# Indirect transfers without padding rows in the last tiles of a graph kernel

## The chip, the cores and the metric

The kernel runs on 1 core of one Trainium2 chip. The metric is the device time in microseconds (us), median of the runs shown. A core has a matrix engine (PE), a vector engine (DVE), a scalar engine (ACT), a general engine (POOL, GpSimd) and a queue engine (SP). Direct DMAs are issued from SP here, indirect ones (gather or scatter by a list of row numbers) from POOL; both run on the core's 16 DMA engines.

## The reference

One layer of attention over the edges of a graph, with a residual and a normalization: 100,000 nodes of 128 float32, 25,000 edges.

```python
dst, src = (edge_index[0], edge_index[1])      # receiver and sender of each edge
edge_feat = concatenate([h[dst], h[src], rel_pos, distance], axis=-1)
x = silu(edge_feat @ W1 + b1)
x = silu(x @ W2 + b2)
scores = (x @ W3 + b3)[:, 0]
mx = segment_max(scores, dst, num_segments=num_nodes)
exp_scores = exp(scores - mx[dst])
den = segment_sum(exp_scores, dst, num_segments=num_nodes)
alpha = exp_scores / (den[dst] + EPS)
msg = h[src] @ Wv * (alpha * node_weight[src])[:, None]
out = segment_sum(msg, dst, num_segments=num_nodes)
return layernorm(x0 + h + out)                 # h is x0, the input
```

## The kernel before

The 25,000 edges are cut into T = 196 tiles of P = 128 edges, four tiles to a group, G = 49 groups. 196 tiles hold EP = 25,088 edges, so 88 places are padding. The padding's sender is node 0, and its receiver is N, past the last node; all 88 come at the end of the edge list, in the last tile, which holds 40 real edges.

The work has three stages, all laid out by hand as a list of steps for each engine:

- Stage 1 (to about 270 us). For each group POOL gathers the senders' rows (`xw`: 128 values and the node's weight, 516 bytes) by `snd_t` into `rec` (kind "hs"); PE transposes them (line 584) and multiplies by the sender half of W1 and by the edge features (lines 577, 578); ACT copies the product beside the gathered row (line 493); SP writes the record of 257 values to `rec_d` in DRAM (`write_rec`, line 343). Beside it DVE sorts the edges by receiver (a sorting network over 98 rows of 256), which gives the tables `id_t`, `kg_t`, `sidx_t` of edge number, receiver and output row. In sorted order the padding again comes last.
- Stage 2 (to about 790 us). In sorted order POOL gathers the receivers' rows of `x` by `kg_t` into `hk` (kind "hk", 512 bytes) and the records by `id_t` into `rr` (kind "r", 1,028 bytes; the profile calls its memory `region`). PE, ACT and DVE compute scores, a softmax over each receiver's run of edges, and the weighted sums, 12 to 13 steps behind; ACT normalizes the finished rows in `hk` (line 530).
- Stage 3. POOL scatters the rows of `hk` by `sidx_t` into `out_rows` (kind "sc", line 426). Only the last edge of a run carries an output row; the other rows go to spare rows of `out_rows` past row N, one for each edge. Runs that cross tiles are combined for all tiles at once and scattered by two closing transfers (line 430): 196 rows, one for each tile, as 128 and 68; both transfers handle 128 rows, and a row whose index is past the bound (`SKIP`) is not written.

Beside stages 1 and 2 the nodes without edges are normalized: SP loads and stores 49 blocks of 1 MB, ACT and DVE normalize them.

POOL's order is fixed by `pool_plan`: all 49 groups "hs"; ten groups "hk"; then "r" and "hk" in turn, and when "hk" is out, the last ten groups of "r" in a row; then 49 groups "sc"; then the closing two. A group is always four transfers of one tile each. POOL waits before a group: "hs" for its place in a ring of 12 (`rec_out`); the first "hk" for the sorted tables; the first "r" for all records written; "r" of group g for the product of line 645 of group g - 12 (`z_ready`); "sc" for the dense rows written, then for its group's result (`res_ready`).

Of the kernel before, what the change touches and what calls it, by code (L numbers as in the profile page):

```python
# [11 lines left out]
P = 128  # L12
N = 100000
E = 25000
H = 128
# [4 lines left out]
T = G * TPG  # L20
XW = H + 1
RW = 2 * H + 1
# [2 lines left out]
NB = -(-N // BN)  # L25
LASTROW = N - BN
NOUT = N + 1 + EP

HS_RING, EF_RING, R_RING, X_RING = 12, 4, 12, 4
HK_SEMS, SC_SEMS, Y_SEMS, FAR_RING = 16, 8, 4, 4  # L30
# [22 lines left out]
SKIP = float(1 << 20)  # L53
MAGIC = float(0x5F3759DF)
FLAT = (T + BT) * P
assert SROWS * SORTW == EP and T <= SORTW and EP < 1 << IDBITS and SROWS < P
assert (HALFN - POSB) >> 8 > 0 and NEGB < 255 << 8 and N - POSB < 255 << 8 and (NEGB - HALFN + 1) >> 8 > 0

# [60 lines left out]
def gnn_kernel(nc, x, xw, snd_nat, rcv_nat, id_nat, signs, iota, ef_flat, w1, b1, w2, b2, w3, b3, wv, eye, out):  # L119
    rec_d = nc.dram_tensor("rec_d", (EP, RW), F32).ap()  # L120
    ef_d = nc.dram_tensor("ef_d", (36, EP), BF16).ap()
    far_d = nc.dram_tensor("far_d", (1, FLAT + P), BF16).ap()
    cont_d = nc.dram_tensor("cont_d", (1, FLAT + P), BF16).ap()
# [6 lines left out]
    with ExitStack() as ctx:  # L130
# [6 lines left out]
        ident = sb("ident", [P, P])  # L137
# [8 lines left out]
        snd_t = sb("snd_t", [P, T], I32)  # L146
        id_t = sb("id_t", [P, T], I32)
        kg_t = sb("kg_t", [P, T], I32)
        sidx_t = sb("sidx_t", [P, T], I32)
        kcol = sb("kcol", [P, T])  # L150
        krow = sb("krow", [P, KROW_RING, GE], BF16)
        fixi = sb("fixi", [P, 2], I32)

        hk = sb("hk", [P, G, TPG, H])
# [12 lines left out]
        dst = sb("dst", [P, BR, 3])  # L167
# [6 lines left out]
        rr = region[:].rearrange("p (r q w) -> p r q w", r=R_RING, q=TPG)  # L174
        at = [0]
# [6 lines left out]
        ef = part(EF_RING * GE // 2).bitcast(BF16).rearrange("p (r e) -> p r e", r=EF_RING)  # L182
# [11 lines left out]
        rec = hflat[:, G * GE - HS_RING * TPG * RW:].rearrange("p (r q w) -> p r q w", r=HS_RING, q=TPG)  # L194
# [35 lines left out]
        fv = late(T)  # L230
        fw = late(T)
        yfix = late(2 * H).rearrange("p (k h) -> p k h", k=2)
        yrow = late(4 * H).rearrange("p (k h) -> p k h", k=4)
        fixf = late(2)

        bank = [ctx.enter_context(nc.psum_tensor(f"bank{n}", [P, GE], F32)) for n in range(8)]
# [10 lines left out]
        hs_in = [sem(f"hs_in{r}") for r in range(HS_RING)]  # L247
        ef_in = [sem(f"ef_in{r}") for r in range(EF_RING)]
        rec_out = [sem(f"rec_out{r}") for r in range(HS_RING)]
        r_in = [sem(f"r_in{r}") for r in range(R_RING)]  # L250
        hk_in = [sem(f"hk_in{r}") for r in range(HK_SEMS)]
# [5 lines left out]
        scattered = [sem(f"scattered{r}") for r in range(SC_SEMS)]  # L257
# [33 lines left out]
        def _(sp):  # L291
# [105 lines left out]
                        sp.wait_ge(stored[r], 16 * len(range(r, NB, X_RING)))  # L397
                    sp.sem_inc(S["dense_written"], 1)
            sp.dma_start(fara, fara_d.to_broadcast((P, T))).then_inc(S["fix_in"], 16)
            for k, (first, n) in enumerate(((0, P), (P, T - P))):  # L400
                sp.dma_start(fixf[0:n, k:k + 1], fixi_d[0:1, first:first + n].rearrange("o t -> t o")).then_inc(S["fix_in"], 16)
            sp.wait_ge(S["parts_ready"], 1)
            for k in range(4):
# [14 lines left out]

        @block.gpsimd
        def _(pool):  # L420
            def gather(to, frm, index, done):
                pool.indirect_dma_start(out=to, out_offset=None, in_=frm,  # L422
                                        in_offset=bass.IndirectOffsetOnAxis(ap=index, axis=0)).then_inc(done, 16)

            def scatter(frm, index, done):
                pool.indirect_dma_start(out=out, out_offset=bass.IndirectOffsetOnAxis(ap=index, axis=0),  # L426
                                        in_=frm, in_offset=None).then_inc(done, 16)

            def scatter_some(frm, index, done):
                pool.indirect_dma_start(out=out, out_offset=bass.IndirectOffsetOnAxis(ap=index, axis=0),  # L430
                                        in_=frm, in_offset=None, bounds_check=N - 1, oob_is_err=False).then_inc(done, 16)

            pool.wait_ge(S["snd_in"], 16)
            for kind, g in pool_plan():
                if kind == "hs":
                    wait_ring(pool, rec_out, g - HS_RING, 16)
                    for q in range(TPG):
                        t = g * TPG + q
                        gather(rec[:, g % HS_RING, q, H:RW], xw, snd_t[:, t:t + 1], hs_in[g % HS_RING])
                elif kind == "hk":  # L440
                    if g == 0:
                        pool.wait_ge(S["tab_ready"], 1)
                        pool.wait_ge(S["efp_out"], 144)
                        pool.wait_ge(S["w36_in"], 144)
                    wait_ring(pool, hk_in, g - HK_SEMS, 16 * TPG)
                    for q in range(TPG):
                        t = g * TPG + q
                        gather(hk[:, g, q, :], x, kg_t[:, t:t + 1], hk_in[g % HK_SEMS])
                elif kind == "r":
                    if g == 0:  # L450
                        for r in range(HS_RING):
                            pool.wait_ge(rec_out[r], 16 * len(range(r, G, HS_RING)))
                        pool.wait_ge(S["rows_out"], 80)
                    wait(pool, "z_ready", g - R_RING + 1)
                    for q in range(TPG):
                        t = g * TPG + q
                        gather(rr[:, g % R_RING, q, :], rec_d, id_t[:, t:t + 1], r_in[g % R_RING])
                else:
                    if g == 0:
                        pool.wait_ge(S["dense_written"], 1)  # L460
                    wait(pool, "res_ready", g + 1)
                    wait_ring(pool, scattered, g - SC_SEMS, 16 * TPG)
                    for q in range(TPG):
                        t = g * TPG + q
                        scatter(hk[:, g, q, :], sidx_t[:, t:t + 1], scattered[g % SC_SEMS])
            pool.wait_ge(S["fix_res"], 1)
            for k in range(2):
                scatter_some(yfix[:, k, :], fixi[:, k:k + 1], S["fix_out"])


        @block.scalar
# [72 lines left out]
        def _(pe):  # L544
# [24 lines left out]
            for i in range(B0):  # L569
                j = i - 2  # L570
                if 0 <= j < G:
# [3 lines left out]
                    for q in range(TPG):  # L575
                        to = bank[2 + j % 4][:, q * P:(q + 1) * P]
                        pe.matmul(to, hsT[:, j % 2, q * P:(q + 1) * P], w1b[:], start=True, stop=False)  # L577
                        ins = pe.matmul(to, ef[0:36, j % EF_RING, q * P:(q + 1) * P], w36[:], start=False, stop=True)  # L578
                    ins.then_inc(S["A_ready"], 1)
                if i < G:  # L580
                    wait_ring(pe, hs_in, i, 16 * TPG)
                    wait(pe, "hsT_ready", i - 1)
                    for q in range(TPG):
                        ins = pe.transpose(bank[i % 2][:, q * P:(q + 1) * P], rec[:, i % HS_RING, q, H:2 * H], ident[:])  # L584
# [16 lines left out]
            for s in range(LAST_STEP):  # L601
                g = s - 3
                if 0 <= g < G:
# [3 lines left out]
                    for q in range(TPG):  # L607
                        n = (g % BATCH) * TPG + q
                        ins = pe.matmul(bank[3][0:BT, 0:P], wz[:, BT - 1 - n:2 * BT - 1 - n], x2[:, q * P:(q + 1) * P],  # L609
                                        start=(n == 0), stop=(last and q == TPG - 1), skip_group_check=True)  # L610
                    ins.then_inc(S["score_done"], 1)
                g = s - 2
# [4 lines left out]
                g = s - 1  # L617
                if 0 <= g < G:
# [4 lines left out]
                    for q in range(TPG):  # L623
                        ins = pe.matmul(bank[1][:, q * P:(q + 1) * P], rr[:, g % R_RING, q, 0:H], ident[:], is_transpose=True,  # L624
                                        start=False, stop=(q == TPG - 1), skip_group_check=True)
                    ins.then_inc(S["mm1_done"], 1)
                for b in range(NBATCH):
                    if batch_end(b) + 5 == s:
                        n = group_tiles(b)
# [3 lines left out]
                g = s - Z_LAG - 1  # L633
                if 0 <= g < G:
                    wait(pe, "zs_ready", g + 1)
                    wait(pe, "y_done", g - 1)
                    for q in range(TPG):
                        ins = pe.matmul(bank[Y_BANKS[g % 2]][:, q * P:(q + 1) * P], zs[:, q * P:(q + 1) * P], wvh[:], start=True, stop=True)  # L638
                    ins.then_inc(S["y_ready"], 1)
                g = s - Z_LAG  # L640
                if 0 <= g < G:
                    wait(pe, "m_ready", g + 1)
                    wait(pe, "zs_ready", g)
                    for q in range(TPG):
                        ins = pe.matmul(bank[5][:, q * P:(q + 1) * P], rr[:, g % R_RING, q, H:2 * H], m_q[:, g % 2, q, :],  # L645
                                        start=True, stop=True)
# [5 lines left out]
            for k in range(2):  # L652
                pe.transpose(bank[k][:, 0:P], yrow[:, 2 * k, :], ident[:])
                ins = pe.transpose(bank[k][:, P:T], yrow[0:T - P, 2 * k + 1, :], ident[0:T - P, 0:T - P])
            ins.then_inc(S["fixT_done"], 1)
            pe.wait_ge(S["fixY_ready"], 1)
            pe.transpose(bank[2][:, 0:P], fv[:, 0:P], ident[:])
            pe.transpose(bank[2][0:T - P, P:2 * P], fv[:, P:T], ident[:]).then_inc(S["fixY_done"], 1)


        @block.vector
        def _(dve):
            vec = nc.vector
            count = [0]

            def link(ins):
                count[0] += 1
                ins.then_inc(S["setup"], 1)
                dve.wait_ge(S["setup"], count[0])
# [316 lines left out]
            for s in range(LAST_STEP):  # L986
# [14 lines left out]
                for b in range(NBATCH):  # L1001
                    if batch_end(b) + 4 == s:
                        softmax_first(b)
                    if batch_end(b) + 6 == s:
                        wait(dve, "alphaT_done", b + 1)
                        n, first = group_tiles(b), b * BATCH % R_RING
# [42 lines left out]
            link(vec.reciprocal(h_, h_))  # L1049
            vec.tensor_tensor(fv, fv, h_, ALU.mult).then_inc(S["fixY_ready"], 1)  # L1050
            link(vec.memset(fixi[:], int(SKIP)))
            vec.tensor_copy(fixi[:, 0:1], fixf[:, 0:1])
            link(vec.tensor_copy(fixi[0:T - P, 1:2], fixf[0:T - P, 1:2]))
            dve.wait_ge(S["fixY_done"], 1)
            vec.tensor_copy(yfix[:, 0, :], bank[2][:, 0:P])
            link(vec.tensor_copy(yfix[0:T - P, 1, :], bank[2][0:T - P, P:2 * P]))
            vec.bn_stats(est[:, 1, 0:2, :].rearrange("p j w -> p (j w)"), yfix.rearrange("p j h -> p h j")).then_inc(S["fix_stats"], 1)
            dve.wait_ge(S["res_ready"], G)
            for _ in chain(("fix_stats", 1), 2, est[:, 1], ers[:, 1], cwe, "chain_f", 0, lambda: None):
# [55 lines left out]
```

## Time and profile before

| | us |
|---|---|
| three runs | 998.05, 998.94, 999.92 |
| median | 998.94 |
| profiled execution, span from first to last instruction | 996.1 |
| POOL busy in it | 752.3 (76%) |
| PE busy | 575.9 (58%) |
| DVE busy | 573.2 (58%) |
| ACT busy | 522.6 (52%) |

The profiled execution is known by its span alone; what lies around the span is in the time of a run and not in the span. Busy time leaves out an engine's gaps between two instructions, so an engine that is never asked to wait can stand well below 100%. The DMA engines are nearly full to about 280 us and almost empty from 743 us on.

### The profile page before, as it was taken

The page shows a single profiled execution, that of the slowest core. Times are in us where ns is not written, and L with a number is a line of the kernel's source. Part 1 is how long each engine was busy: PE and PEld are TensorE (multiplying, and loading weights), DVE is VectorE, ACT ScalarE, POOL GpSimd, SP SyncE. Part 2 cuts the span into 40 slices and gives each one's busy share as a digit, 9 for nine tenths or more (in the row PEclk, how much of TensorE's full clock was granted, in tenths as well). Part 3 has the DMA queues.
Part 4 walks back from the last instruction along what each step waited for, and adds up shares of the span by engine and source line. Part 5 has one row for each costly group of instructions (what it writes and reads, how often), then busy time and mean ns, then how long its engine had stood idle before and what let it go on. Part 6 is the DMA issues. An engine that isn't in the chain of part 4 may idle for free.

```text
span 996.1 us, 10941 instructions
## 1 busy us (share of the span) xinstructions
PE 575.9 (58%) x2587; PEld 394.8 (40%) x2587; DVE 573.2 (58%) x2275; ACT 522.6 (52%) x1168; POOL 752.3 (76%) x790
## 2 busy tenths in 40 slices
PE   0989999988704457677667666777996600000000
PEld 0656766665502223455445444545675500000000
DVE  6987887773452737597698987953678841000000
ACT  0356655554523756777698979974786630000000
POOL 6777777777777777777777777777777777777777
PEclk9999999999998776788788988878999855555555
DMA  7799999989965877788778878763452231111111
GB/s 208 227 302 315 321 320 333 336 233 311 330 226 161 288 256 245 273 292 268 273 272 283 292 234 317 246 185 91 129 124 79 71 78 53 53 51 52 53 53 45
DMA packets 85079, 206.12 MB, mean 207 GB/s; under 512 B 19797, under 2 KB 56566, under 8 KB 72472
## 3 DMA queue, kind: packets, MB, share of 16 engines
q1 hardware_dynamic: 56728, 140.95, 41.7%
q0 software_dynamic: 28288, 64.48, 22.8%
q8 instruction: 21, 0.34, 0.1%
q14 instruction: 42, 0.34, 0.1%
HBM read 113.16 MB, written 92.31 MB: 206 GB/s over the span
## 4 chain that ended last, share of the span: by engine, by line
POOL 38%; issue 23%; PE 20%; ACT 13%; DVE 5%; DMA 0%; POOLq 0%; ACTq 0%; DVEq 0%
POOL hk L422 23%; POOL out_rows L426 15%; ACT xin L478 6%; PE bank L622 5%; PE bank L638 4%; PE bank L645 3%; PE bank L624 2%; ACT hk L530 2%; PE bank L616 2%; PE bank L609 2%; ACT hkT L501 1%; ACT x L511 1%; ACT zs L521 1%; PE bank L597 1%; DVE dst L899 1%
## 5 line engine op out<-in xcount | busy, mean ns | idle before, releaser
L478 ACT ACTIVATE xin<-xin,drs 128x128 f32<-128x128 f32 x637 | 258.1, 484 | 51.6 <-DVE drs L884 51.5
L422 POOL DMA_INDIRECT hk<-in_xw,snd_t x196 | 188.0, 959 | 62.0 <-issue 59.4
L426 POOL DMA_INDIRECT out_rows<-hk,sidx_t x196 | 188.8, 963 | 59.7 <-issue 59.4
L422 POOL DMA_INDIRECT region<-rec_d,id_t x196 | 186.8, 953 | 59.7 <-issue 59.1
L422 POOL DMA_INDIRECT hk<-in_x,kg_t x196 | 186.6, 952 | 59.7 <-issue 59.7
L899 DVE BATCH_NORM_STATS2 dst<-xin 128x6 f32<-128x256 f32 x392 | 137.0, 414 | 61.6 <-DMA xin<-in_x 61.0
L577 PE MATMUL bank<-w1b,region 128*128 128x128 f32 x392 | 149.1, 484 | 13.8 <-ACT region L488 7.8
L622 PE MATMUL bank<-hkT,w1a 128*128 128x512 f32 x98 | 73.2, 839 | 138.8 <-issue 98.3
L577 PEld LDWEIGHTS bank<-w1b,region 128*128 128x128 f32 x392 | 99.8, 315 | 33.9 <-ACT region L488 10.1
L622 PEld LDWEIGHTS bank<-hkT,w1a 128*128 128x128 f32 x98 | 20.1, 240 | 175.5 <-issue 163.2
L511 ACT ACTIVATE x<-bank,bcol 128x512 f32<-128x512 f32 x49 | 33.5, 683 | 95.0 <-PE bank L624 95.0
L530 ACT ACTIVATE hk<-hk,ers 128x128 f32<-128x128 f32 x196 | 79.6, 483 | 0.8 <-DVE ers L884 0.8
L488 ACT ACTIVATE region<-bank 128x512 f32<-128x512 f32 x49 | 28.9, 589 | 91.4 <-PE bank L584 91.4
L584 PE MATMUL bank<-ident,hk 128*128 128x128 f32 x196 | 54.3, 433 | 21.6 <-DMA w<-hk 16.8
L638 PE MATMUL bank<-wvh,zs 128*128 128x128 f32 x392 | 63.7, 314 | 4.1 <-ACT zs L521 4.1
L967 DVE TENSOR_SCALAR m_q<-krow,kcol,acol 128x128 f32<-128x128 bf16 x196 | 62.4, 354 | 4.6 <-PE bank L645 4.4
L609 PE MATMUL bank<-x,wz 128*16 128x128 f32 x392 | 55.5, 289 | 15.4 <-ACT x L506 9.6
L616 PE MATMUL bank<-x,w2s 128*128 128x512 f32 x98 | 59.0, 686 | 6.8 <-ACT x L511 4.7
L638 PEld LDWEIGHTS bank<-wvh,zs 128*128 128x128 f32 x392 | 57.8, 226 | 6.3 <-ACT zs L521 5.5
L645 PE MATMUL bank<-m_q,region 128*128 128x128 f32 x392 | 57.6, 296 | 0.0
L578 PE MATMUL bank<-w,region 36*128 36x128 bf16 x196 | 55.6, 284 | 0.0
L645 PEld LDWEIGHTS bank<-m_q,region 128*128 128x128 f32 x392 | 54.5, 215 | 0.0
(176 smaller groups left out, 853.0 us busy)
## 6 DMA issues: line engine op xcount, KB each, us to landing
xin<-in_x SPq DMA_DIRECT2D x49, 1024.0 KB, 8.2
out_rows<-xin SPq DMA_DIRECT2D x49, 1024.0 KB, 5.2
rec_d<-hk SPq DMA_DIRECT2D x49, 514.0 KB, 7.7
krow<-seg_d SPq DMA_DIRECT2D x49, 128.0 KB, 3.5
hk<-in_xw,snd_t POOLq DMA_INDIRECT x196, 5.8
hk<-in_x,kg_t POOLq DMA_INDIRECT x196, 3.9
region<-rec_d,id_t POOLq DMA_INDIRECT x196, 3.6
out_rows<-hk,sidx_t POOLq DMA_INDIRECT x196, 2.2
```

What stands on the lines that cost most here:

```text
L422: pool.indirect_dma_start(out=to, out_offset=None, in_=frm, in_offset=bass.IndirectOffsetOnAxis(ap=index, axis=0)).then_inc(done, 16)
L426: pool.indirect_dma_start(out=out, out_offset=bass.IndirectOffsetOnAxis(ap=index, axis=0), in_=frm, in_offset=None).then_inc(done, 16)
L478: ins = nc.scalar.activation(xin[:, j % X_RING, n, :], xin[:, j % X_RING, n, :], ACT.Identity, bias=drs[:, j % 2, 1, n:n + 1], scale=drs[: ...
L530: ins = nc.scalar.activation(hk[:, g, q, :], hk[:, g, q, :], ACT.Identity, scale=ers[:, b % 2, 0, n:n + 1], bias=ers[:, b % 2, 1, n:n + 1])
L577: pe.matmul(to, hsT[:, j % 2, q * P:(q + 1) * P], w1b[:], start=True, stop=False)
L609: ins = pe.matmul(bank[3][0:BT, 0:P], wz[:, BT - 1 - n:2 * BT - 1 - n], x2[:, q * P:(q + 1) * P], start=(n == 0), stop=(last and q == TPG ...
L616: pe.matmul(bank[2][:], w2s[:], x1[:], start=True, stop=True).then_inc(S["mm2_done"], 1)
L622: pe.matmul(bank[1][:], w1a[:], hkT[:, g % 2, :], start=True, stop=False, skip_group_check=True)
L638: ins = pe.matmul(bank[Y_BANKS[g % 2]][:, q * P:(q + 1) * P], zs[:, q * P:(q + 1) * P], wvh[:], start=True, stop=True)
L645: ins = pe.matmul(bank[5][:, q * P:(q + 1) * P], rr[:, g % R_RING, q, H:2 * H], m_q[:, g % 2, q, :], start=True, stop=True)
L899: ins = vec.bn_stats(dst[:, n:n + 2, :].rearrange("p j w -> p (j w)"), xin[:, j % X_RING, n:n + 2, :].rearrange("p j h -> p h j"))
L967: ins = vec.tensor_scalar(m_q[:, g % 2, q, :], krow[:, g % KROW_RING, q * P:(q + 1) * P], kcol[:, t:t + 1], acol[:, b % 2, n:n + 1], ALU.i ...
```

## The change

The row count of nine indirect transfers of the 786 is cut, and the padding of the senders is laid out to match. The gathers by sender take 127, 125, 124 and 48 rows in the last group, and the host places the 25,000 edges accordingly (the padding places lie at the ends of those four tiles). The last tile of the gathers of x, of the record gathers and of the scatters takes 40 rows. The closing two transfers take 112 and 84 rows (all 196 tiles, split elsewhere, and no unused rows). The number of transfers and their order stay.

```diff
+HS_ROWS = [P] * (T - 4) + [127, 125, 124, 48]
+LAST_ROWS = E - (T - 1) * P
+FIX_ROWS = 112, T - 112
...
-            for k, (first, n) in enumerate(((0, P), (P, T - P))):
+            for k, (first, n) in enumerate(((0, FIX_ROWS[0]), FIX_ROWS)):
...
+            def rows_in(t):
+                return LAST_ROWS if t == T - 1 else P
...
-                        gather(rec[:, g % HS_RING, q, H:RW], xw, snd_t[:, t:t + 1], hs_in[g % HS_RING])
+                        n = HS_ROWS[t]
+                        gather(rec[0:n, g % HS_RING, q, H:RW], xw, snd_t[0:n, t:t + 1], hs_in[g % HS_RING])
...
-                        gather(hk[:, g, q, :], x, kg_t[:, t:t + 1], hk_in[g % HK_SEMS])
+                        n = rows_in(t)
+                        gather(hk[0:n, g, q, :], x, kg_t[0:n, t:t + 1], hk_in[g % HK_SEMS])
...
-                        gather(rr[:, g % R_RING, q, :], rec_d, id_t[:, t:t + 1], r_in[g % R_RING])
+                        n = rows_in(t)
+                        gather(rr[0:n, g % R_RING, q, :], rec_d, id_t[0:n, t:t + 1], r_in[g % R_RING])
...
-                        scatter(hk[:, g, q, :], sidx_t[:, t:t + 1], scattered[g % SC_SEMS])
+                        n = rows_in(t)
+                        scatter(hk[0:n, g, q, :], sidx_t[0:n, t:t + 1], scattered[g % SC_SEMS])
...
-            for k in range(2):
-                scatter_some(yfix[:, k, :], fixi[:, k:k + 1], S["fix_out"])
+            for k, n in enumerate(FIX_ROWS):
+                scatter_some(yfix[0:n, k, :], fixi[0:n, k:k + 1], S["fix_out"])
...
-            pe.transpose(bank[2][:, 0:P], fv[:, 0:P], ident[:])
-            pe.transpose(bank[2][0:T - P, P:2 * P], fv[:, P:T], ident[:]).then_inc(S["fixY_done"], 1)
+            pe.transpose(bank[2][0:FIX_ROWS[0], 0:P], fv[:, 0:FIX_ROWS[0]], ident[:])
+            pe.transpose(bank[2][0:FIX_ROWS[1], P:2 * P], fv[:, FIX_ROWS[0]:T], ident[:]).then_inc(S["fixY_done"], 1)
...
+    at = np.concatenate([t * P + np.arange(n) for t, n in enumerate(HS_ROWS)])
     rcv = np.full(EP, N, src.dtype)
-    rcv[:E] = src
+    rcv[at] = src
     snd = np.zeros(EP, dst.dtype)
-    snd[:E] = dst
+    snd[at] = dst
```

On POOL, from the start of the gathers by sender to the first record gathers; ahead of the change the rows are (target, source and index, rows x values):

```order
L422 DMA hk<-in_xw,snd_t 128x129 x196
L422 DMA hk<-in_x,kg_t 128x128 x40
L422 DMA region<-rec_d,id_t 128x257 x4
```

and with it:

```order
L429 DMA hk<-in_xw,snd_t 128x129 x192
L429 DMA hk<-in_xw,snd_t 127x129
L429 DMA hk<-in_xw,snd_t 125x129
L429 DMA hk<-in_xw,snd_t 124x129
L429 DMA hk<-in_xw,snd_t 48x129
L429 DMA hk<-in_x,kg_t 128x128 x40
L429 DMA region<-rec_d,id_t 128x257 x4
```

Nothing moved; four of the 196 have other row counts. Further down on POOL, from the last gathers of x to the end, with the change:

```order
L429 DMA hk<-in_x,kg_t 128x128 x3
L429 DMA hk<-in_x,kg_t 40x128
L429 DMA region<-rec_d,id_t 128x257 x39
L429 DMA region<-rec_d,id_t 40x257
L433 DMA out_rows<-hk,sidx_t 125089x128 x196
L437 DMA out_rows<-xin,fixi 125089x128 x2
```

Here too the order is the same; for a scatter the listed shape is that of the whole target, so its row count doesn't show.

## Rows read from the trace of the kernel before

**Rows 1.** The page's head and busy time: us (share of span) xinstructions.

```profile
span 996.1 us, 10941 instructions
...
PE 575.9 (58%) x2587; PEld 394.8 (40%) x2587; DVE 573.2 (58%) x2275; ACT 522.6 (52%) x1168; POOL 752.3 (76%) x790
```

**Rows 2.** Groups by line on POOL: busy us, mean ns | idle before, what ended it.

```profile
L426 POOL DMA_INDIRECT out_rows<-hk,sidx_t x196 | 188.8, 963 | 59.7 <-issue 59.4 <-ACT hk L530 0.3
L422 POOL DMA_INDIRECT hk<-in_xw,snd_t x196 | 188.0, 959 | 62.0 <-issue 59.4 <-DMA snd_t<-in_snd_nat 2.6
L422 POOL DMA_INDIRECT region<-rec_d,id_t x196 | 186.8, 953 | 59.7 <-issue 59.1 <-PE bank L645 0.6
L422 POOL DMA_INDIRECT hk<-in_x,kg_t x196 | 186.6, 952 | 59.7 <-issue 59.7
L430 POOL DMA_INDIRECT out_rows<-xin,fixi x2 | 2.0, 986 | 0.6 <-issue 0.6
L1105 POOL MEMSET const-uint8-127<- 128x1 uint8 x1 | 0.1, 120 | 0.0
...
L1105 POOL MEMSET const-float32-0.0<- 128x1 f32 x1 | 0.1, 99 | 0.2 <-issue 0.2
```

**Rows 3.** Waits of POOL: who, for what, us in total, times, longest.

```profile
POOL hk L422 <- DMA snd_t<-in_snd_nat: 2.6, 1, 2.6
POOL region L422 <- PE bank L645: 0.6, 2, 0.3
...
POOL out_rows L426 <- ACT hk L530: 0.3, 1, 0.3
```

**Rows 4.** Lines 422, 426: ns min/median/max, first and last start in us.

```profile
L422 POOL DMA_INDIRECT hk<-in_xw,snd_t x196: 940/945/1310, 3.0 to 249.5; - x196
L422 POOL DMA_INDIRECT hk<-in_x,kg_t x196: 940/945/1097, 250.7 to 692.0; - x196
L422 POOL DMA_INDIRECT region<-rec_d,id_t x196: 942/947/1092, 300.8 to 742.4; - x196
...
L426 POOL DMA_INDIRECT out_rows<-hk,sidx_t x196: 954/958/1268, 743.6 to 990.9; - x196
```

**Rows 5.** Order of time on POOL, the end: start us, us, what [idle before].

```profile
989.60 0.96 POOL L426 DMA_INDIRECT out_rows<-hk,sidx_t  x1 [0.30 <-issue]
990.86 0.96 POOL L426 DMA_INDIRECT out_rows<-hk,sidx_t  x1 [0.30 <-issue]
992.13 0.99 POOL L430 DMA_INDIRECT out_rows<-xin,fixi  x1 [0.30 <-issue]
993.42 0.98 POOL L430 DMA_INDIRECT out_rows<-xin,fixi  x1 [0.30 <-issue]
```

**Rows 6.** DMA queues from 980 to 990 us: packets, MB, share of 16 engines.

```profile
DMA packets 249, 0.52 MB, mean 52 GB/s; under 512 B 122, under 2 KB 122, under 8 KB 249
...
q0 software_dynamic: 249, 0.52, 16.6%
```

**Rows 7.** Order of time, 736 to 739 us: PE, then POOL.

```profile
736.21 1.06 PE L645 MATMUL bank<-m_q,region 128*128 128x128 f32 x8
...
738.58 1.00 POOL L422 DMA_INDIRECT region<-rec_d,id_t  x1 [0.30 <-issue]
```

**Rows 8.** Around 250 us: order of time, queues, landings, line 422's durations.

```profile
244.50 0.94 POOL L422 DMA_INDIRECT hk<-in_xw,snd_t  x1 [0.30 <-issue]
...
258.03 1.11 PE L584 MATMUL bank<-ident,hk 128*128 128x128 f32 x4
...
271.98 0.90 SPq L343 DMA_DIRECT2D rec_d<-hk  x1
...
q1 hardware_dynamic: 2761, 5.65, 85.7%
q0 software_dynamic: 579, 1.19, 17.8%
...
L422 POOL DMA_INDIRECT hk<-in_xw,snd_t x17: 940/945/947, 219.5 to 239.5; - x17
...
DMA to landing us min/median/max: 4.3/6.8/10.0
...
DMA to landing us min/median/max: 6.9/9.2/11.7
```

**Rows 9.** Order of time on ACT: the closing result, before the closing transfers.

```profile
827.14 0.88 ACT L538 ACTIVATE xin<-xin,ers 128x128 f32<-128x128 f32 x2 [10.11 <-DVE ers L884]
```

**Rows 10.** Waits, all engines: PE's longest.

```profile
PE bank L622 <- DMA region<-rec_d,id_t: 32.9, 1, 32.9
```

More of the change, by code:

```diff
@@ L55 @@
 FLAT = (T + BT) * P
+assert sum(HS_ROWS) == E and 0 < LAST_ROWS <= P
 assert SROWS * SORTW == EP and T <= SORTW and EP < 1 << IDBITS and SROWS < P
@@ L1051, in _ @@
             link(vec.memset(fixi[:], int(SKIP)))
-            vec.tensor_copy(fixi[:, 0:1], fixf[:, 0:1])
-            link(vec.tensor_copy(fixi[0:T - P, 1:2], fixf[0:T - P, 1:2]))
+            for k, n in enumerate(FIX_ROWS):
+                ins = vec.tensor_copy(fixi[0:n, k:k + 1], fixf[0:n, k:k + 1])
+            link(ins)
             dve.wait_ge(S["fixY_done"], 1)
-            vec.tensor_copy(yfix[:, 0, :], bank[2][:, 0:P])
-            link(vec.tensor_copy(yfix[0:T - P, 1, :], bank[2][0:T - P, P:2 * P]))
+            for k, n in enumerate(FIX_ROWS):
+                ins = vec.tensor_copy(yfix[0:n, k, :], bank[2][0:n, k * P:(k + 1) * P])
+            link(ins)
             vec.bn_stats(est[:, 1, 0:2, :].rearrange("p j w -> p (j w)"), yfix.rearrange("p j h -> p h j")).then_inc(S["fix_stats"], 1)
@@ L1071 @@
     dst = np.asarray(dst)
+    at = np.concatenate([t * P + np.arange(n) for t, n in enumerate(HS_ROWS)])
     rcv = np.full(EP, N, src.dtype)
-    rcv[:E] = src
+    rcv[at] = src
     snd = np.zeros(EP, dst.dtype)
-    snd[:E] = dst
+    snd[at] = dst
     ef = np.zeros((4, EP), np.float32)
-    ef[0:3, :E] = np.asarray(edge_attr_3).T
-    ef[3, :E] = np.asarray(edge_weight1)[:, 0]
+    ef[0:3, at] = np.asarray(edge_attr_3).T
+    ef[3, at] = np.asarray(edge_weight1)[:, 0]
     def nat(a):
```

## The prediction

> **What bounds the kernel now.** Start with the page's head and its line of busy engines [rows 1]: the span is 996.1 us, and POOL is the busiest engine with 752.3 us, yet only 76%. The groups by line [rows 2] show why 76% is full: its work is four times 196 indirect transfers and two closing ones, and nearly all the idle time before them ends by "issue", that is, nobody was waited for. The waits of POOL [rows 3] confirm it: one real wait, 2.6 us for the first index load; the waits on PE and ACT are 0.3 us each, the same gap that stands before every transfer. The durations by line [rows 4] complete the chain: the first gather starts at 3.0 us, and in the closing stretch [rows 5] each instruction starts 1.26 us after the one before. 786 instructions of 0.95 to 0.99 us with a gap of 0.30 us fill 3.0 to 994.4 us (991.4 us, 1.261 us each), and 1.7 us is left for the last landing and the end. So the kernel is a queue of 786 transfers on one engine, and a nanosecond saved on any of them is saved at the end, unless POOL then has to wait for somebody.
>
> **What the change does to the sum.** No transfer goes away: the 786 gaps of 0.30 us stay (236 us), and so does everything on the other engines (the copies and transposes of the closing step change their row counts, and end at 828 us [rows 9], 164 us before POOL reaches the closing transfers; cost nothing, and something only if that cover of 164 us were gone). What changes is the row count of nine transfers: 127, 125, 124 and 48 in the last group of gathers by sender (88 rows fewer), 40 in the last tile of the gathers of x by receiver, of the records and of the scatters (88 fewer each), and 112 and 84 for the closing two (16 and 44 fewer). Together 412 rows.
>
> The price of a row on POOL is the unknown: every transfer of the trace handles 128 rows. Bounds from the nearest rows:
> - Lower end nothing. Records of 1,028 bytes take 947 ns and rows of 512 bytes 945 ns [rows 4], so bytes are free, and the whole may be a fixed cost. The bounds check of the closing transfers adds 28 ns over 128 rows (986 against 958), 0.22 ns a row: some work per row is very cheap. At that price 412 rows are 0.09 us.
> - Upper end everything by the row: 945/128 = 7.38 ns for 264 rows, 958/128 = 7.48 for 88, 986/128 = 7.70 for 60, together 3.1 us.
> - Below nothing: a count that doesn't divide well could be dearer; that is a rival below.
>
> I take a fixed part as large as POOL's smallest instructions, the MEMSETs of 99 to 120 ns [rows 2], say 110 ns, and let the rest go by steps of sixteen rows, since the tail shows a full transfer leave as 16 equal packets of 4,096 bytes, 8 rows each (249 packets in 10 us, 127 of them data, for 8 transfers) [rows 6]. Then a step costs (945 - 110)/8 = 104 ns. Counts 127, 125 and 124 still need 8 steps and save nothing; 48 and the three 40s need 3 and save 5 each; 112 saves 1 and 84 saves 2. That is 23 steps, **2.4 us**. I choose the upper half because nothing in the trace shows a large fixed part besides the 0.30 us gap; but this choice is the weak step.
>
> The Trainium skill speaks against it. In DMA: Bandwidth & Descriptors, section Anatomy of one DMA, it calls descriptor generation a small and variable part, of which a lot can be emitted before the incremental cost shows. By that the sum would be near the lower end; no row here varies the count, so the trace can't decide.
>
> **Is there room for the gain?** A gather of records for group g may only start when PE has finished the product of line 645 for group g - 12. For the last group this margin is the smallest: PE ends at 736.21 + 1.06 = 737.27 us, POOL starts at 738.58 [rows 7], 1.31 us. Ahead of that point lie the savings of the senders (0.52 us) and of x (0.52 us): 1.04 us, at the upper end 1.3 us. It just fits, so nothing is lost. The rest (records, scatters, closing: 1.36 us) comes behind it. The scatters wait for ACT's results, of which the first wait is a plain gap [rows 3].
>
> **Could late data cost anything?** If a short gather leaves over fewer rings, it lands late. In the quiet tail software packets took 16.6% of 16 engines over 10 us, 26.6 us for 1,016 rows, 26 ns a row [rows 6]; 127 rows behind each other are 3.3 us. Between 240 and 260 us the hardware queue takes 86% of the engines beside it [rows 8], so 7 us (half the ring) to 20 us (its 17.8%) are possible. The 127-row gather starts at 244.50 us; PE uses its group at 258.03 us [rows 8], and would be up to 8 us late. Behind PE stands the last record write at 271.98 us, landing in 11.7 us at worst [rows 8], hence by 284; POOL needs it at 300.8 us [rows 4]. 17 us of cover are more than 8, and PE itself idles 32.9 us for the first record gather [rows 10]. Cost zero.
>
> **The rivals.**
> 1. **A fixed cost** (chance 0.34). POOL pays some 945 ns whatever the count. For: bytes don't matter, the check is almost free. Gain 0 to under 2.0 us; by the 0.22 ns per row 0.09 us, so 998.85 us.
> 2. **Few rings, slow rows** (0.18). Rows are dealt out evenly, so a transfer may use only as many rings, up to 16, as divide its rows: 127 one, 125 five, 124 four, 48 sixteen, 40 ten, 112 sixteen, 84 fourteen. If POOL writes one row of every ring per step, steps are rows per ring: 127, 25, 31, 3, 4 (three times), 7 and 6 where 8 stood: +119 +17 +23 -5 -12 -1 -2 = +139 steps. A step costs between 28/8 = 3.5 ns (the check alone) and 104 ns, so +0.5 to +14.5 us; I take the geometric middle, 19 ns, +2.6 us, 1001.6 us. It decides for slower (over 2.0 us) from 14.4 ns a step. It takes place at 244.5 to 248 us, in three instructions. A ring that is full would act alike: 8 transfers in flight (longest landing 10.0 us with no instruction over 947 ns [rows 8]) were held, 72 entries a ring; 127 more on one ring is beyond what is seen. Against it: a scatter's target has 125,089 rows, an odd number, and still leaves over 16 packets [rows 6].
> The Trainium skill gives this rule in the same page, section Why a DMA increments its semaphore by 16 and not by 1: the largest number up to 16 that divides the slowest dimension of both sides, with 127 partitions on one engine. For scatters the trace disagrees on the DRAM side; for gathers no row shows it.
> 3. **Few rings, cheap rows** (0.06). The same split, but POOL's cost lies in serving rings: the three odd counts fall to near 110 ns, 3 x 0.84 = 2.5 us more gained, some 5 us, 994.0 us.
>
> **How the numbers follow.** The forecast (0.42) is 2.4 us off the span, 996.1 to 993.7 us. The runs' median of 998.94 us lies 2.8 us above the profiled span; carried over, 996.5 us, its own range 995.0 to 997.8. The upper bound of the gain (3.1 us) and the runs' spread of 0.9 us set the low end at 995.0; the high end takes in the fixed cost and the lower half of rival 2, 1001.6. Left out: rival 3 and the upper half of rival 2, 0.15. A measurement of this kernel tells 0.2% (2.0 us) from no change. Faster: 0.42 + 0.06 = 0.48; slower: rival 2 above 14.4 ns, 0.14; the rest, 0.38, is the same.
>
> **What would show it.** In the trace after, the scatters of 40 rows should take some 0.44 us instead of 0.96, the gather of 48 rows 0.42, the closing two 0.88 and 0.78, and 127, 125 and 124 rows 0.94 as before. Unchanged durations mean rival 1. An instruction of over 1.1 us at 244 to 248 us means rival 2. POOL's gaps must stay at 0.30 us, and no wait on PE may appear at 738 us. The forecast is wrong if the price per row is under 4.9 ns (2.0/412), or if POOL waits for a ring.

## The result: slower by a quarter of a per cent

| | us, median | runs | lowest to highest |
|---|---|---|---|
| before | 999.76 | 10 | 998.05 to 1001.7 |
| after | 1002.23 | 10 | 1001.04 to 1003.89 |

The ratio is 1.0026, 95% interval 1.0017 to 1.0035: slower by 1.7 to 3.5 us. That is small, but the interval leaves 1 out. Forecast were 996.5 us, a range of 995.0 to 1001.6 us, and a gain of 2.4 us. There are 88 rows less in each of four series, and the kernel is slower.

### The profile page after: what moved, and what is told of

Its sections match the earlier page's. It is cut to its first block, busy times and chain, and to the rows that moved or that the text cites. A ratio compares the mean times of both kernels' runs of the same rounds, so it can differ in the third digit from the quotient of the medians.

```text
span 999.4 us, 10941 instructions
## 1 busy us (share of the span) xinstructions
PE 574.3 (57%) x2587; PEld 395.9 (40%) x2587; DVE 572.6 (57%) x2275; ACT 522.0 (52%) x1168; POOL 755.3 (76%) x790
## 4 chain that ended last, share of the span: by engine, by line
POOL 44%; issue 22%; PE 18%; ACT 10%; DVE 5%; DMA 0%; POOLq 0%; ACTq 0%; DVEq 0%
POOL hk L429 26%; POOL out_rows L433 15%; ACT xin L489 4%; PE bank L633 4%; PE bank L649 4%; PE bank L656 3%; POOL region L429 3%; ACT hk L541 2%; PE bank L627 2%; PE bank L635 2%; PE bank L620 2%; DVE dst L910 1%; ACT hkT L512 1%; ACT zs L532 1%; ACT L527 1%
## 5 line engine op out<-in xcount | busy, mean ns | idle before, releaser
L429 POOL DMA_INDIRECT hk<-in_xw,snd_t x196 | 191.1, 975 | 62.0 <-issue 59.5
L620 PE MATMUL bank<-x,wz 128*16 128x128 f32 x392 | 55.7, 289 | 17.4 <-ACT x L517 9.4
L987 DVE TENSOR_TENSOR hk<-bank,hk 128x512 f32<-128x512 f32 x49 | 33.5, 683 | 45.1 <-PE bank L649 45.1
```

What stands on the lines that cost most here:

```text
L429: pool.indirect_dma_start(out=to, out_offset=None, in_=frm, in_offset=bass.IndirectOffsetOnAxis(ap=index, axis=0)).then_inc(done, 16)
```

## The profile after

The head and the busy times of the changed kernel, which answer to [rows 1]. The span grew by 3.3 us and POOL's busy time by 3.0 us; nobody else's changed by more than 1.6 us.

```profile
span 999.4 us, 10941 instructions
...
PE 574.3 (57%) x2587; PEld 395.9 (40%) x2587; DVE 572.6 (57%) x2275; ACT 522.0 (52%) x1168; POOL 755.3 (76%) x790
```

POOL's groups by line (busy us, mean ns | idle before, what ended it) answer to [rows 2]. Look at the mean: the gathers by sender went from 188.0 to 191.1 us, the other three series stand within 0.1 us of before, and the idle times are the same to 0.4 us. So the loss sits inside one series' instructions, not in a wait.

```profile
L429 POOL DMA_INDIRECT hk<-in_xw,snd_t x196 | 191.1, 975 | 62.0 <-issue 59.5 <-DMA snd_t<-in_snd_nat 2.5
L433 POOL DMA_INDIRECT out_rows<-hk,sidx_t x196 | 188.8, 963 | 59.7 <-issue 59.4 <-ACT hk L541 0.3
L429 POOL DMA_INDIRECT region<-rec_d,id_t x196 | 186.7, 953 | 60.1 <-issue 58.9 <-PE bank L656 1.3
L429 POOL DMA_INDIRECT hk<-in_x,kg_t x196 | 186.6, 952 | 59.8 <-issue 59.8
```

POOL in order of time at the change (start us, us, what [idle before]) answers to the first line of [rows 8]:

```profile
245.41 0.94 POOL L429 DMA_INDIRECT hk<-in_xw,snd_t  x1 [0.30 <-issue]
246.66 2.56 POOL L429 DMA_INDIRECT hk<-in_xw,snd_t  x1 [0.30 <-issue]
249.52 1.20 POOL L429 DMA_INDIRECT hk<-in_xw,snd_t  x1 [0.30 <-issue]
251.02 1.30 POOL L429 DMA_INDIRECT hk<-in_xw,snd_t  x1 [0.30 <-issue]
252.63 0.89 POOL L429 DMA_INDIRECT hk<-in_xw,snd_t  x1 [0.30 <-issue]
253.83 0.95 POOL L429 DMA_INDIRECT hk<-in_x,kg_t  x1 [0.31 <-issue]
```

The gathers of 127, 125 and 124 rows take 2.56, 1.20 and 1.30 us where 128 rows take 0.94; the one of 48 rows takes 0.89. From the start of the first to the start of what follows it is 7.17 us, against 5.00 us before: 2.17 us lost in four instructions, and the gap stays at 0.30 us. The end of the same view, for [rows 5]:

```profile
993.04 0.96 POOL L433 DMA_INDIRECT out_rows<-hk,sidx_t  x1 [0.31 <-issue]
994.30 0.91 POOL L433 DMA_INDIRECT out_rows<-hk,sidx_t  x1 [0.30 <-issue]
995.52 0.99 POOL L437 DMA_INDIRECT out_rows<-xin,fixi  x1 [0.30 <-issue]
996.82 0.95 POOL L437 DMA_INDIRECT out_rows<-xin,fixi  x1 [0.30 <-issue]
```

The scatter of 40 rows saves 0.05 us, not 0.52, and the closing two of 112 and 84 rows 0.03 at best. The short transfers save almost nothing; the odd ones cost a lot. What the forecast left out or sized wrongly is all in these ten lines. What they can't show is the law behind it: they hold few counts, and the dear ones stand in one place.

## The experiments

Two theories stand against each other at first. A "ring" stands here for one of the up to 16 equal shares into which a transfer's rows are dealt: a full scatter leaves as 16 packets of 8 rows [rows 6]. A: a transfer uses as many rings as the largest number up to 16 that divides its rows, and POOL pays a fixed 855 ns and some 13.4 ns for each row of the fullest ring (48 rows, 3 a ring: 888 ns; 128, 8: 945; 125, 25: 1,196; 124, 31: 1,303; 127, 127: 2,562). B: the loss has another place. C, D, E and P are rivals on parts of A. The names of the experiments stand for the edits below, which are made to the changed kernel. The first four compute the whole result; the last two leave part of it out, and ran once each. All are compared with before on one chip; its median there was 998.33 us in 27 runs for the first four, and 998.36 us in 20 runs for the last two.

**Only the gathers by sender** (e1):

```diff
-LAST_ROWS = E - (T - 1) * P
-FIX_ROWS = 112, T - 112
+LAST_ROWS = P
+FIX_ROWS = P, T - P
```

(and the closing scatters with all 128 rows, as before)

> Only the last group of gathers by sender has 127, 125, 124 and 48 rows; all else is as before. Theory A (few rings: POOL writes one row of every ring per step, and a transfer uses the largest number of rings up to 16 that divides its rows): the four instructions last 2.56, 1.20, 1.30 and 0.89 us again, 2.2 us more than four of 0.945, so the ratio to before is 1.0022. Theory B (the odd counts are harmless here and the loss of the changed kernel comes from elsewhere, the short tiles in sorted order or later waits on PE): ratio 1.000, and the 127-row gather near 0.95 us.

Measured: 999.97 us, ratio 1.0020, interval 1.0010 to 1.0029. In order of time:

```profile
245.83 2.55 POOL L429 DMA_INDIRECT hk<-in_xw,snd_t  x1 [0.31 <-issue]
248.69 1.20 POOL L429 DMA_INDIRECT hk<-in_xw,snd_t  x1 [0.30 <-issue]
250.20 1.30 POOL L429 DMA_INDIRECT hk<-in_xw,snd_t  x1 [0.30 <-issue]
251.80 0.88 POOL L429 DMA_INDIRECT hk<-in_xw,snd_t  x1 [0.30 <-issue]
```

The four instructions are the same to 10 ns, and bring the loss alone. B falls.

**All but the odd counts** (e2):

```diff
-HS_ROWS = [P] * (T - 4) + [127, 125, 124, 48]
+HS_ROWS = [P] * (T - 1) + [40]
```

> The changed kernel with 128, 128, 128 and 40 rows in the last group of gathers by sender, so only the odd counts are undone. Theory A: all instructions at 0.92 to 0.95 us, the five short ones save 0.03 to 0.06 us each, 0.2 us in all: ratio to before 0.9998, not to be told from 1. Theory B: ratio stays near 1.0026.

Measured: 998.07 us, ratio 0.9999, interval 0.9990 to 1.0008. The rest of the change, with the same 412 rows saved, is worth nothing that can be measured. Its last three transfers (the scatter of 40 rows and the closing two) read, in order of time:

```profile
991.44 0.92 POOL L433 DMA_INDIRECT out_rows<-hk,sidx_t  x1 [0.30 <-issue]
992.66 0.98 POOL L437 DMA_INDIRECT out_rows<-xin,fixi  x1 [0.30 <-issue]
993.95 0.94 POOL L437 DMA_INDIRECT out_rows<-xin,fixi  x1 [0.30 <-issue]
```

**The same 88 rows off the same four gathers, with counts that divide well** (e3):

```diff
-HS_ROWS = [P] * (T - 4) + [127, 125, 124, 48]
+HS_ROWS = [P] * (T - 4) + [120, 112, 96, 96]
```

> The changed kernel with the same 88 rows taken off the same four gathers by sender, as 120, 112, 96 and 96 rows (15, 16, 16 and 16 rings, 8, 7, 6 and 6 rows on each). Theory A: 0.95, 0.93, 0.92 and 0.92 us, 0.06 us less than four full ones, ratio to before 0.9997. Theory C (any count other than 128 is dear on POOL, whatever divides it): the four take over 1.1 us each, ratio 1.001 or more.

Measured: 998.63 us, ratio 1.0002, interval 0.9993 to 1.0011. In order of time:

```profile
246.96 0.99 POOL L429 DMA_INDIRECT hk<-in_xw,snd_t  x1 [0.30 <-issue]
248.26 0.95 POOL L429 DMA_INDIRECT hk<-in_xw,snd_t  x1 [0.30 <-issue]
249.51 0.92 POOL L429 DMA_INDIRECT hk<-in_xw,snd_t  x1 [0.30 <-issue]
250.73 0.91 POOL L429 DMA_INDIRECT hk<-in_xw,snd_t  x1 [0.30 <-issue]
```

C falls: none takes over 1.1 us. 120 rows take 0.99 us (A said 0.95), 112 rows as much as a full one, 96 rows 0.03 us less. A count need not be 128; it must divide.

**Sixteen gathers of 127 rows in a row** (e4):

```diff
-HS_ROWS = [P] * (T - 4) + [127, 125, 124, 48]
+HS_ROWS = [P] * (T - 17) + [127] * 16 + [56]
```

> The changed kernel with sixteen gathers by sender of 127 rows ahead of the last one (56 rows, 14 rings of 4). Theory A: each of the sixteen takes 2.56 us, 1.62 us more than a full one, whatever stands around it: 25.8 us more than before, ratio 1.026. Theory D (the 2.56 us of the one gather were a wait for room in a ring, a matter of what was in flight there): after each other they wait for their ring's transfer of 127 rows of 516 bytes, so durations differ from one to the next and grow past 3.3 us, some 16 x 3 = 48 us, ratio 1.04 or more.

Measured: 1025.51 us against 998.33, ratio 1.0271, interval 1.0251 to 1.0291; 27 us against 25.8 of A and 48 of D. Line 429 between 230 and 270 us (ns min/median/max, then landings), and the middle of the row:

```profile
L429 POOL DMA_INDIRECT hk<-in_xw,snd_t x14: 2536/2541/2561, 230.2 to 269.3; - x14
...
DMA to landing us min/median/max: 8.3/10.8/15.0
```

```profile
247.31 2.54 POOL L429 DMA_INDIRECT hk<-in_xw,snd_t  x1 [0.30 <-issue]
250.15 2.54 POOL L429 DMA_INDIRECT hk<-in_xw,snd_t  x1 [0.31 <-issue]
255.10 2.54 POOL L429 DMA_INDIRECT hk<-in_xw,snd_t  x1 [2.41 <-issue]
```

All are within 25 ns of each other while transfers land 8 to 15 us after their start. A wait for something in flight would differ from one to the next, so the instruction's time is POOL's own work. D falls for the durations. One gap of 2.41 us in the middle is a thing of its own: it explains 2.1 us of the 27, the trace names no releaser, and its cause stays open (a shortage of room wasn't tested; the other eight of these gathers show no such gap).

This run also shows what the empty rings do. Its page's count of DMA packets, with the same line of before above it:

```profile
DMA packets 85079, 206.12 MB, mean 207 GB/s; under 512 B 19797, under 2 KB 56566, under 8 KB 72472
...
DMA packets 88914, 206.03 MB, mean 201 GB/s; under 512 B 23667, under 2 KB 60436, under 8 KB 76306
```

There are 3,870 small packets more, though less is moved. The 127 rows of such a gather leave as 16 packets, fifteen of 8 rows and one of 7. If each of the fifteen rings without rows sends 16 packets beside them, that makes 240 for each gather, 3,840 for sixteen. Listed singly, the packets of the software queue (q0) up to 300 us say so: 3,600 of 32 bytes and 240 of 28, that is, 4 bytes for each of 8 or of 7 rows. So a ring without rows still gets an entry of 4 bytes for every row of the fullest ring.

**The price by itself, gathers** (e5; every second one of the senders' gathers in tiles 61 to 159 takes fewer rows):

```diff
+COUNTS = (127, 126, 125, 124, 123, 122, 121, 119, 117, 113, 112, 96, 80, 64, 63, 62, 61, 48, 40, 32, 31, 16, 15, 8, 17)
+READ_ROWS = [P] * 60 + [COUNTS[(t // 2) % 25] if t % 2 else P for t in range(100)] + [P] * 36
...
-                        n = HS_ROWS[t]
+                        n = READ_ROWS[t]
```

> Leaves out part of the senders' rows: in tiles 61 to 159 every second gather by sender takes only n rows, n going twice through 127, 126, 125, 124, 123, 122, 121, 119, 117, 113, 112, 96, 80, 64, 63, 62, 61, 48, 40, 32, 31, 16, 15, 8, 17. It measures the price by itself. Theory A, from 128 rows (8 on a ring, 945 ns), 48 (3, 888), 125 (25, 1196), 124 (31, 1303) and 127 (127, 2562): about 855 ns and 13.4 ns for each row of the fullest ring. So 113 rows (one ring) 2.37 us, 123 (3 rings of 41) 1.40, 122 (2 of 61) 1.67, 61 (one ring) 1.67 as well, 31 (one) 1.27, 17 (one) 1.08, 126 (14 of 9) 0.97, 121 (11 of 11) 1.00, 16 and 8 (one row each ring) 0.87. Theory E (the price goes with the number of rows times the lack of rings, or with the number of rings): 61 and 122 rows would differ, and 8 and 15 rows would differ from 16 by more than 0.05 us. Theory P (a price per row, the forecast's): 64 rows 0.53 us, 16 rows 0.21.

**The same for scatters** (e6, in tiles 41 to 189):

```diff
+WRITE_ROWS = [P] * 40 + [COUNTS[(t // 2) % 25] if t % 2 else P for t in range(150)] + [P] * 6
...
-                        n = rows_in(t)
+                        n = WRITE_ROWS[t]
                         scatter(hk[0:n, g, q, :], sidx_t[0:n, t:t + 1], scattered[g % SC_SEMS])
```

> Leaves out part of the output rows: in tiles 41 to 189 every second scatter writes only n rows, the same list of n three times. The stretch has almost no other DMA. Theory A: as for the gathers and 13 ns more, so 127 rows 2.57 us, 61 and 122 rows 1.68, 16 rows 0.88, though the target has 125,089 rows, which no number up to 16 divides but 1, 7 and 11, 13: only the tile's side counts. If the target's side counted too, 128 rows could not take 0.96 us. Landing of 127 rows: 26 ns a row behind each other, 3.3 us of transfer where 8 rows take 0.2, so 2.2 - 0.96 + 2.57 + 3.1 = 6.9 us from start to landing.

(The expectation has its divisors wrong: no number from 2 to 16 divides 125,089. If the target's side counted, every scatter would have one ring.)

As whole runs, e5 took 1011.8 us and e6 1018.87, 13.4 and 20.5 us more than before. A's prices for the shortened transfers sum to 12.3 and 17.4 us, and e6 also keeps the three odd gathers by sender, 2.2 us.

Fifteen of the 25 counts, the lower of the two gathers of a count and the median of its three scatters, in ns; "A" is 855 + 13.4 x rows per ring:

| rows | rings x rows each | A | gather | scatter |
|---|---|---|---|---|
| 127 | 1 x 127 | 2557 | 2548 | 2546 |
| 113 | 1 x 113 | 2369 | 2369 | 2362 |
| 122 | 2 x 61 | 1672 | 1667 | 1668 |
| 61 | 1 x 61 | 1672 | 1662 | 1662 |
| 123 | 3 x 41 | 1404 | 1402 | 1400 |
| 124 | 4 x 31 | 1270 | 1295 | 1324 |
| 62 | 2 x 31 | 1270 | 1267 | 1278 |
| 31 | 1 x 31 | 1270 | 1267 | 1262 |
| 119 | 7 x 17 | 1083 | 1082 | 1077 |
| 17 | 1 x 17 | 1083 | 1080 | 1074 |
| 126 | 14 x 9 | 976 | 980 | 986 |
| 64 | 16 x 4 | 909 | 903 | 904 |
| 48 | 16 x 3 | 895 | 871 | 876 |
| 16 | 16 x 1 | 868 | 852 | 847 |
| 8 | 8 x 1 | 868 | 884 | 876 |

Some of the scatters, in order of time:

```profile
867.86 2.55 POOL L435 DMA_INDIRECT out_rows<-hk,sidx_t  x1 [0.30 <-issue]
...
874.59 1.19 POOL L435 DMA_INDIRECT out_rows<-hk,sidx_t  x1 [0.30 <-issue]
...
883.29 1.67 POOL L435 DMA_INDIRECT out_rows<-hk,sidx_t  x1 [0.30 <-issue]
...
913.75 1.66 POOL L435 DMA_INDIRECT out_rows<-hk,sidx_t  x1 [0.31 <-issue]
917.01 0.88 POOL L435 DMA_INDIRECT out_rows<-hk,sidx_t  x1 [0.30 <-issue]
...
927.30 0.85 POOL L435 DMA_INDIRECT out_rows<-hk,sidx_t  x1 [0.30 <-issue]
```

These are 127, 125, 122, 61, 48 and 16 rows. The pairs decide: 122 and 61 rows take the same, and so do 62 and 31, 119 and 17; twice or seven times the rows at the same number on a ring cost nothing. That is A, to some 30 ns, for the other ten counts too (112 rows: 933 and 938 where A says 949; 125 rows: 1193 and 1187 where A says 1190); only the scatters of 124 rows lie further off. Taking the lower of two gathers leaves out single slow ones, of which 31 rows had the longest, 1,536 ns. P falls (16 rows would be 0.21 us, and are 0.85), and so does E in its first form. Its second form holds in small: 8 and 15 rows take 20 to 30 ns more than 16, so a transfer of fewer than 16 rings pays about 25 ns besides, and 124 rows take 50 ns more than A says in the scatters, for which I have no reason. A short transfer also makes the full one behind it dearer: in the scatters a full one takes 958 ns behind a full one, 972 behind a shorter one on 16 rings and 987 behind one on fewer (medians), 0.01 and 0.03 us that A doesn't have. That the target's 125,089 rows don't matter is shown too, and so it is for gathers: `xw` has 100,000 rows, which 7 doesn't divide, and 119 rows take 1,082 ns (7 rings), not the 2,450 of one ring. The landing of the 127-row scatter, its line's rows in the window of that one instruction:

```profile
L435 POOL DMA_INDIRECT out_rows<-hk,sidx_t x1: 2546/2546/2546, 867.9 to 867.9; - x1
...
DMA to landing us min/median/max: 7.0/7.0/7.0
```

7.0 us where 6.9 were expected, against 2.2 for a full one.

How many rings carry data can be seen directly. In the changed kernel, between 995.7 and 996.9 us, only the data of the 40-row scatter move (DMA view). Of 32 packets 22 are small (six of them have 16 bytes, 4 for each of 4 rows), and 10 have 2 KB, 4 rows each; a full scatter has 16 packets with rows, 8 in each.

```profile
DMA packets 32, 0.02 MB, mean 17 GB/s; under 512 B 22, under 2 KB 22, under 8 KB 32
```

For the other counts the sizes of e6's packets decide it, listed singly from 744 us on. Theory A says for each count how many rings carry rows and how many rows each has; with packets of up to 8 rows, and 4 bytes a row on the other rings, the 196 scatters should send 2,401 packets of 4,096 bytes, 57 of 2,560, 48 of 1,024 and 2,751 of 32. The trace has exactly these numbers. So the split isn't only inferred from durations: POOL's time grows with the fullest ring, and as many entries leave on the empty rings as on that one. That POOL's time goes into writing them is the reading that fits; the trace doesn't look inside an instruction.

The Trainium skill's rule on the number of engines (DMA: Bandwidth & Descriptors, section Why a DMA increments its semaphore by 16 and not by 1) speaks of the slowest dimension of both sides. Here the tile's side decides alone, by the largest divisor up to 16: a full scatter has 16 rings though its target has 125,089 rows. With the rule's example of 127 on one engine the runs agree (2.55 us, one ring).

## Why the prediction was wrong

**What bounds the kernel: right.** POOL's queue sets the end. E4 is the cleanest proof: 1.6 us put into each of sixteen instructions, 25.5 us in all, and 2.1 us of one gap came out as 27 us at the end. PE idled 38 us there for the first record gather, as it did 33 us before, and POOL waited 1.6 us for PE in the whole run (0.6 before).

**The price of a row: the step that failed.** The forecast took 110 ns as fixed, from the MEMSETs, and spread the other 835 ns over 8 steps of sixteen rows, 104 ns each. The runs show some 850 ns fixed and 13.4 ns a step. Its 23 steps, forecast at 2.4 us, give 0.3 us at that price. The rows at hand held a hint that I weighed too low: bytes for free and a bounds check of 28 ns over 128 rows meant that work per row is cheap here. A MEMSET of 0.1 us was no measure for the fixed part of an indirect transfer. The Trainium skill's sentence (DMA: Bandwidth & Descriptors, section Anatomy of one DMA) that many descriptors can be emitted before the incremental cost shows fits the counts that 16 divides: from 128 rows down to 16 the gather goes from 945 to 852 ns. It doesn't fit 127 rows, 2.55 us.

**"Counts 127, 125 and 124 save nothing and cost nothing": wrong**, and this is where the sign turned. They cost 1.62 + 0.25 + 0.36 = 2.2 us. Rival 2 had the mechanism, with its +139 steps. Its size it had too high: 19 ns a step where 13.4 were measured, less than the 14.4 from which it would have decided for slower. At 13.4 ns a step its own sum is +1.9 us. The trace's seven changed instructions before the closing two give 2.23 - 0.06 - 2 x 0.03 - 0.05 = 2.1 us, within the interval of 1.7 to 3.5. That the measured time lies near rival 2's 1001.6 us is in part luck, as the next paragraph shows. Rival 2 stood at 0.18 since I held the scatter's odd target against it; that argument was unsound, as that side doesn't count.

**The range** ended at rival 2's middle, 1001.6, and the time is 1002.23. Part of it is the base: the 10 runs of before have a median of 999.76, 0.8 us above the three that were shown. From the base that was shown, a loss of 1.9 to 2.5 us would have ended at 1000.8 to 1001.4, inside.

**The room for the gain** wasn't needed, and is thinner than said. In the changed kernel one record gather waits for PE at 742 us, which answers to [rows 7]; below it stands the same gather in e3, where no count changes its instruction by more than 0.05 us:

```profile
741.99 0.95 POOL L429 DMA_INDIRECT region<-rec_d,id_t  x1 [0.64 <-PE bank L656]
...
739.88 0.94 POOL L429 DMA_INDIRECT region<-rec_d,id_t  x1 [0.86 <-PE bank L656]
```

That is 0.34 us over the plain gap in one and 0.56 in the other, while e2 and before have no such wait. So the margin of 1.31 us, read from one execution, differs by more than its own size from one to the next, and a gain of 1.04 us ahead of this point could not be counted on.

The profiled span grew by 3.3 us: 0.9 stood already at 246.66 us before the first odd gather (the 192 gathers before it are the same work; single instructions differ there from run to run), 2.2 are the four gathers, 0.3 this wait, less 0.1 of short ones. Of these only the 2.2 are shown to be the change's.

**Late landing: right, no cost.** PE waited 0.90 us for the last group of senders, where up to 8 us were allowed for:

```profile
259.81 1.11 PE L595 MATMUL bank<-ident,hk 128*128 128x128 f32 x4 [0.90 <-DMA hk<-in_xw,snd_t]
```

and POOL's first record gather, at 303.9 us, followed without a wait.

## What to carry to other kernels

Where a queue of indirect transfers bounds a kernel, its time is the number of transfers (0.30 us gap and some 0.85 us each here), not their rows: dropping padding saves 13 ns for each row that the fullest ring loses. Choose the row count of an indirect transfer as a multiple of 16, and never one without a large divisor up to 16: an instruction with 127 rows takes 2.7 times as long as one with 128, and in the quiet stretch its data land 4.8 us later. Padding a tile up to 128 is the cheap choice, and when a trace never varies a quantity, a change that varies it deserves a wide range on both sides.

## What the runs showed of the hardware

- POOL's time for an indirect transfer: about 855 ns + 13.4 ns x rows on the fullest ring, the same for gathers of 516-byte rows and scatters of 512-byte rows, from 8 to 127 rows (e5, e6; to 30 ns, but 50 for scatters of 124); with fewer than 16 rings 15 or 8 rows take about 25 ns more than 16 do.
- The rings used are the largest divisor up to 16 of the tile's rows, whatever the tensor in DRAM has (packet sizes in e6). Rings without rows carry 4 bytes for each row of the fullest ring: 32 bytes beside each packet of 8 rows.
- Sixteen gathers of 127 rows, landing up to 15 us after their start, didn't lengthen an instruction of POOL; one gap of 2.41 us among them is unexplained.
